# A grouped convolution in blocks of 16 positions of one group, the edges of two groups in one matrix, and tiles of one group of 16 rows

## What is computed

```python
# x (128, 32, 512), cond (128, 128), conv weight (32, 8, 9): 4 groups of 8 channels, 9 taps
y = conv_general_dilated(x, weight, (1,), [(4, 4)], ('NCH','OIH','NCH'), feature_group_count=4)
y = y + einsum('nd,od->no', cond, c_weight)[:, :, None] + bias[None, :, None]
base = einsum('btd,od->bto', y, base_W) + base_b            # 512 -> 512
logits = einsum('btd,nd->btn', y, router_W) + router_b      # 15 routes
p, i = top_k(softmax(logits), 8)
w = sum over k of p[k] * onehot(expert_map[i[k]])           # (.., 8 experts)
h = einsum('btd,erd->bter', y, A)                           # 8 experts x rank 16
out = x + base + einsum('bter,eor->bto', h * w[..., None], B) * 2
```

## Time and profile before

| | |
|---|---|
| median of 3 runs | 197.27 us (197.12 to 205.5) |
| profiled execution | 197.38 us, span 195.6 us |
| granted TensorE clock, mean | 0.991 |
| TensorE busy | 187.3 us, 96%, 1297 matmuls |
| VectorE busy | 161.1 us, 82% |
| ScalarE busy | 76.9 us, 39% |
| GpSimd busy | 139.1 us, 71% |
| moved | 27.66 MB, mean 141 GB/s |

### The profile page before, as it was taken

One profiled execution on the slowest core, in us unless ns is written; L12 is line 12 of the kernel. 1 busy time (PEld: TensorE's weight loads), 2 busy tenths in 40 slices (PEclk: granted clock), 3 DMA queues, 4 the chain that ended last, 5 costly groups with the idle time before them and its releaser, 6 DMA issues.

```text
span 195.6 us, 4329 instructions
## 1 busy us (share of the span) xinstructions
PE 187.3 (96%) x1297; PEld 180.1 (92%) x1297; DVE 161.1 (82%) x547; ACT 76.9 (39%) x197; POOL 139.1 (71%) x115
## 2 busy tenths in 40 slices
PE   7899699999999999999999999999999999998993
PEld 2788599999999999999999999999999999997992
DVE  0899987888889888889888889888898889775663
ACT  3674434434333444433334444343344443122210
POOL 4539796777887777777887777778877777943520
PEclk9999969999999999999999999999999999999999
DMA  5985442455444434445443335444334133333312
GB/s 180 312 292 214 111 140 80 159 167 162 146 124 124 152 116 153 162 162 157 125 140 123 134 130 162 162 162 147 137 110 150 71 86 111 107 107 109 111 54 107
DMA packets 19051, 27.66 MB, mean 141 GB/s; under 512 B 2144, under 2 KB 9696, under 8 KB 19040
## 3 DMA queue, kind: packets, MB, share of 16 engines
q1 hardware_dynamic: 18576, 27.05, 42.6%
q10 hardware_dynamic: 432, 0.48, 0.7%
q0 software_dynamic: 32, 0.01, 0.2%
HBM read 19.14 MB, written 8.39 MB: 141 GB/s over the span
## 4 chain that ended last, share of the span: by engine, by line
PE 83%; DVE 8%; DMA 4%; issue 2%; ACT 1%; DVEq 0%; ACTq 0%
PE wide_ps L516 53%; PE conv_banks L498 15%; PE wide_ps L540 10%; DMA wide_sb<-wide_w 2%; DMA x_in<-x_first 2%; PE hwt_bank L527 2%; PE conv_banks L516 1%; DVE terms L672 1%; DVE y_rows L647 1%; DVE xr L642 1%; DVE wide_lo L757 1%; DVE y L731 1%; DVE spread L703 0%; DVE expert_w L707 0%; ACT wide_hi L324 0%
## 5 line engine op out<-in xcount | busy, mean ns | idle before, releaser
L516 PE MATMUL wide_ps<-wide_hi,y_hi 128*128 128x400 f32 (+1 forms) x248 | 80.4, 329 | 1.1 <-DVE xr L642 0.8
L516 PE MATMUL wide_ps<-wide_lo,y_hi 128*128 128x400 f32 (+1 forms) x248 | 77.1, 315 | 0.0
L516 PE MATMUL wide_ps<-wide_hi,y_lo 128*128 128x400 f32 (+1 forms) x248 | 76.8, 314 | 0.0
L437 POOL TENSOR_TENSOR terms_lo<-terms,terms_hi 128x768 fp32r<-128x768 f32 x28 | 51.6, 1842 | 31.8 <-ACT terms_hi L345 31.8
L516 PEld LDWEIGHTS wide_ps<-wide_hi,y_hi 128*128 128x128 f32 x248 | 46.6, 189 | 3.5 <-issue 1.0
L516 PEld LDWEIGHTS wide_ps<-wide_lo,y_hi 128*128 128x128 f32 x248 | 46.9, 190 | 0.0
L516 PEld LDWEIGHTS wide_ps<-wide_hi,y_lo 128*128 128x128 f32 x248 | 46.6, 189 | 0.0
L432 POOL TENSOR_TENSOR xr<-xr,biases_sb 128x512 f32<-128x512 f32 x32 | 41.3, 1291 | 5.6 <-DMA xr<-x_rows 5.5
L443 POOL TENSOR_TENSOR y_lo<-y,y_hi 128x512 fp32r<-128x512 f32 x31 | 40.2, 1295 | 3.3 <-ACT y_hi L352 3.3
L359 ACT ACTIVATE hw_hi<-hwt_bank 128x128 fp32r<-128x128 f32 x31 | 8.6, 277 | 81.7 <-PE hwt_bank L527 81.7
L352 ACT ACTIVATE y_hi<-y 128x512 fp32r<-128x512 f32 x32 | 20.2, 632 | 17.9 <-PE wide_ps L516 16.8
(11 more groups left out here) (93 smaller groups left out, 256.3 us busy)
## 6 DMA issues: line engine op xcount, KB each, us to landing
xr<-x_rows SPq DMA_DIRECT2D x32, 256.0 KB, 2.7
out<-xr SPq DMA_DIRECT2D x31, 256.0 KB, 2.0
even<-x_even SPq DMA_DIRECT2D x28, 132.0 KB, 2.6
terms<-x_odd SPq DMA_DIRECT2D x28, 128.0 KB, 2.8
wide_sb<-wide_w SPq DMA_DIRECT2D x4, 328.0 KB, 5.1
x_in<-x_first SPq DMA_DIRECT2D x2, 260.0 KB, 4.3
x_in<-x_pair SPq DMA_DIRECT2D x1, 520.0 KB, 5.9
biases_sb<-biases SPq DMA_DIRECT2D x1, 263.5 KB, 4.3
```

The source lines that it names most:

```text
L437: nc.gpsimd.tensor_tensor(terms_lo[i % 2][:, :, :, :], terms[i][:, :, :, :], terms_hi[i % 2][:, :, :, :].bitcast(F32), ALU.subtract)\
L516: mm = nc.tensor.matmul(sums_of(t, k)[:, b, 0:columns[1] - columns[0]], a[k % 2][:, r, :], w[:, r, columns[0]:columns[1]], start=r == 0 an ...
```

## The change

A block is now 16 positions of the 8 channels of one group, which is 128 partitions again, and a tile is one group of 16 batches (16 x 32 blocks = 512 columns). Output block and input block have the same size, and since 9 taps reach only 4 positions to each side, the second matrix is nearly empty: shifted by 8 positions for the even groups, each output block needs its own input block (W_OWN) and, in one half of its positions only, a neighbour (W_REACH). Per tile there are two products of 256 columns, (W_OWN + W_REACH) on shared blocks and W_OWN on the loaded difference; the third product, the edge, is nonzero in one half of the output partitions only, and the edges of an even and an odd group lie in one matrix (W_QUARTERS): one product for two tiles. So an even tile has nine matmuls of 256 columns, an odd one six.

VectorE subtracts one term a tile (`difference`), and one edge term every second step (`edge`, both operands from SBUF). `condition` waits for the whole convolution and is three additions, each waiting for the one before: the shared sum and the condition; the other sum and the shared rows; the edge sum and the shared rows of 64 partitions. `turn` waits for the last. The common sum's own semaphore is gone. The edge sums lie in the bank of the transposed `hw`, and `turn_hw` now waits for the condition of tile t + 3. ScalarE and GpSimd split 512 + 256/2 elements a tile instead of 768. SyncE loads 256 KB a tile and 256 KB of edges for two, after the low parts of the same step.

The start is written anew: four tiles directly, convolution weights in five pieces (14 matrices instead of 4), condition weights and the expert map loaded on ScalarE's queue, the comparison with the experts' numbers by eight small operations on VectorE, placed ahead of the first condition, and `hw_low(0)` in step 0. Steps 1 to 28 have one convolution each. Keep-warm matmuls between the first convolutions and the first front are 3 instead of 4.

```diff
+            def conv(t, g, p):
+                h = g % 2
+                pe.wait_ge(terms_lo_ready, t - START + 1)
+                parts = [(conv_ps[:, h, 0, :, :], W_SUM[g], terms_hi[h][:, 1], terms_lo[h][:, 1]),
+                         (conv_ps[:, h, 1, :, :], W_OWN[g], terms_hi[h][:, 0], terms_lo[h][:, 0])]
                 if h == 0:
+                    pe.wait_ge(y_rows_ready, t)
+                    parts.append((edge_ps, W_QUARTERS[g // 2], edge_hi, edge_lo))
+                else:
+                    pe.wait_ge(y_rows_ready, t - 1)
...
             def turn_hw(t, k):
+                if from_tile(t, 1) and up_to_tile(t, TILES - 4):
+                    pe.wait_ge(y_rows_ready, t + 4)
...
-                if from_tile(t, 1) and up_to_tile(t, TILES - 5):
-                    conv(t, k, p)
+                if from_tile(t, 1) and up_to_tile(t, TILES - 4):
+                    conv(t + 3, (k + 3) % GROUPS, p + 2)
...
+            def condition(t, g, q):
+                h = g % 2
+                shared, other = 1 - h, h
+                rows = y_rows[h]
+                reached = slice(EDGE, P) if h == 0 else slice(0, EDGE)
+                dve.wait_ge(conv_done, t + 1)
+                c = cond_sb[:, g, bass.ds(q * Q, Q)]
+                nc.vector.tensor_tensor(rows[:, :, shared, :], conv_ps[:, h, 0, :, :],
+                                        c.unsqueeze(2).to_broadcast([P, Q, MK]), ALU.add)\
                     .then_inc(common_ready, 1)
+                dve.wait_ge(common_ready, t - START + 1)
+                nc.vector.tensor_tensor(rows[:, :, other, :], conv_ps[:, h, 1, :, :],
+                                        rows[:, :, shared, :], ALU.add).then_inc(own_ready, 1)
+                dve.wait_ge(own_ready, t - START + 1)
+                nc.vector.tensor_tensor(rows[reached, :, shared, :], edge_ps[reached],
+                                        rows[reached, :, shared, :], ALU.add)\
                     .then_inc(y_rows_ready, 1)
...
+            def difference(t, i):
+                dve.wait_ge(odd_ready, t - START + 1)
+                nc.vector.tensor_tensor(terms[i][:, 0, :, :], terms[i][:, 0, :, :], odd_ps,
+                                        ALU.subtract).then_inc(differences_ready, 1)
+            def edge(p, j):
+                dve.wait_ge(edges_loaded[j], (p - START // 2 - j) * 8 + 16)
+                nc.vector.tensor_tensor(edges[j][:, 0, :, :], edges[j][:, 0, :, :],
+                                        edges[j][:, 1, :, :], ALU.subtract).then_inc(edge_ready, 1)
...
             wide_low(0)
+            dve.wait_ge(map_ready, 1)
+            for e in range(E):
+                nc.vector.tensor_scalar(is_expert[:, e, :], map_f[:, :], float(e), None,
+                                        ALU.is_equal).then_inc(is_expert_ready, 1)
+            bias_condition(0)
+            condition_first(0)
+            turn(0, 0)
...
+            def step(t, k, p, q):
+                if isinstance(t, int) and t < START - 2:
+                    condition_first(t + 2)
+                elif up_to_tile(t, TILES - 3):
+                    condition(t + 2, (k + 2) % GROUPS, q + (k + 2) // GROUPS)
...
+                if up_to_tile(t, TILES - 5):
+                    difference(t + 4, k)
+                    if k % 2 == 1 and up_to_tile(t, TILES - 7):
+                        edge(p + 3, 1 - k // 2)
...
# SyncE, in each step
                     sync.wait_ge(terms_lo_ready, t + 1)
+                    load_terms(t + 8, k % URING)
+                    if k % 2 == 0:
+                        sync.wait_ge(edge_lo_ready, p + 1)
+                        load_edges(p + 4, k // 2)
```

More of the change, by code:

```diff
@@ L470, in keep_warm, with conv_first @@
                     nc.tensor.matmul(bank, zeros[:, 0:P], zeros[:, :], start=True, stop=True)
-            def conv_first(sums, i, h, products):
+            X_HIGH, X_W_REST, X_REST = (conv_hi, x_hi), (conv_lo, x_hi), (conv_hi, x_lo)
+            def conv_first(t, products=(X_HIGH, X_W_REST, X_REST)):
                 for w, a in products:
-                    for b in range(BLOCKS):
-                        mm = nc.tensor.matmul(sums, w[:, h, b, :], a[i][:, h, :, b:b + M],
-                                              start=w is conv_hi and a is x_hi and b == 0,
-                                              stop=a is x_lo and b == BLOCKS - 1)
-                return mm
@@ new lines @@
+    blocks = []
+    for g in range(GROUPS):
+        first = (1 - g % 2) * BP // 2
+        own = quads[:, g, :, :, first:first + BLKI * BP].reshape(N // Q, Q, CG, BLKI, BP)
+        blocks.append(own.transpose(0, 4, 2, 1, 3).reshape(N // Q, P, Q, BLKI))
+    blocks = np.stack(blocks, axis=1)
+    units, edges = [], []
+    for g in range(0, GROUPS, 2):
+        even, odd = blocks[:, g], blocks[:, g + 1]
+        units += [np.stack([even[..., 0:BLK:2], even[..., 1:BLK:2]], axis=2),
+                  np.stack([odd[..., 2:BLKI:2], odd[..., 1:BLKI:2]], axis=2)]
+        edges.append(np.stack([
+            np.concatenate([even[:, :EDGE, :, 2:BLKI:2], odd[:, EDGE:, :, 0:BLK:2]], axis=1),
+            np.concatenate([even[:, :EDGE, :, 1:BLK:2], odd[:, EDGE:, :, 1:BLKI:2]], axis=1)],
+            axis=2))
@@ L860 @@
+    units = np.stack(units[:GROUPS], axis=1).reshape(TILES, P, 2, Q, MK)
+    edges = np.stack(edges, axis=1).reshape(TILES // 2, P, 2, Q, MK)
     w = np.asarray(L0_cond_weight)
-    conv = np.zeros((BP, CH, HALVES, BLOCKS, BP, CH), w.dtype)
-    for b in range(BLOCKS):
+    conv = np.zeros((W_ALL, BP, CG, BP, CG), w.dtype)
+    for g in range(GROUPS):
+        own_w = w[g * CG:(g + 1) * CG].transpose(2, 1, 0)
+        later = g % 2 * BP // 2
         for s in range(BP):
             for r in range(BP):
-                tap = BP * b + s - r
+                tap = s - r + later
@@ L866 @@
                 if 0 <= tap < TAPS:
[L867 to L874 removed]
+                    conv[W_OWN[g], s, :, r] = conv[W_SUM[g], s, :, r] = own_w[tap]
```

529 lines of the change are left out of this document (262 added, 267 removed).

## The result

| | before | after |
|---|---|---|
| median | 197.19 us (196.28 to 205.5) | 204.65 us (204.61 to 204.67, 4 runs) |
| ratio, 95% interval | | 1.0394 [1.0359, 1.0429] |
| profiled execution, span | 197.38, 195.6 | 204.66, 202.5 |
| first front matmul of tiles 1, 2, 3, 4 | 17.33, 27.08, 33.56, 39.08 | 20.29, 26.55, 34.48, 40.46 |
| of tile 28 | 172.11 | 178.95 |

The kernel became 3.9% slower, and the medians lie 7.5 us apart. (The 205.5 is one slow execution, which the ratio leaves out.) The span grew by 6.9. Until the front of tile 4 it is 1.38 us late, the 24 steps from there to tile 28 take 138.49 us instead of 133.03 (+5.46), and the end 23.55 instead of 23.49. The other 0.4 lies outside the span (2.16 instead of 1.78).

The account below looks back on a forecast made before the run. The prediction took two loops of nearly one length, TensorE's work (5.54 us) and the ring (5.48), as bounds. 195.6 + 0.6 (loop) - 0.2 (start) = 196.0 span, plus 1.8 around it: 197.8 us, range 194.6 to 201.2.

Parts of the forecast that it names:

- the start: Everything up to the third front: front 1 later, at 19.4, front 2 earlier, at 25.2; - 0.2 us, between - 3 and + 3.
- the end: The work after the loop: the same as before, 0 us.
- The ring: Front matmuls, logits, routing, output addition, next front: 5.48 us a step, not shortened by the diff, limiting any gain to 1.6.
- the rival that TensorE binds: Rival (a), in the loop: TensorE binds, all 5.0 us of removed matmuls come out, 192.6 us; chance 0.07.
- VectorE's chain with an edge difference: From the condition's start through additions, turn and differences to the logits, with the edge difference every second step: 2.59 us.
- VectorE's chain without it: From the condition's start through three additions, turn and differences to the logits, in steps without an edge difference: 2.26 us.
- The slower rival: Rival (b): dependent additions (0.11 gaps) or a turn of 0.85 cost more, 202 us; decides from 0.28 on; chance 0.13.
- When the condition can start: VectorE sees the convolution's end 5.74 us after the front's start with nine matmuls, 5.38 with six.
- two loops: In the kernel before: TensorE's own work, 5.54 us, and the path front matmuls, logits, routing, output addition, next front, 5.48.
- The map's delay: In the start: the expert map's conversion is ready at 9.2, so the first turn ends at 11.9 against 9.82 before.
- The 0.3 that I allowed for the clock: In the start: 0.3 us for a lowered TensorE clock, since the new step 2 has idle time like that before.
- The signs that the prediction gave for too short a chain: In the loop: the turn's row over 0.75 us, or gaps between the three additions over 0.1.

Follow-up runs that it names:

- twice a step: Kernel before the change, with both differences of a unit reading the odd blocks from SBUF instead of their PSUM copy: 221.49 us, ratio 1.1237.
- the last kernel: Changed kernel with edge differences and map comparisons on GpSimd, the first addition early, and the output addition ahead of the hw product: 191.91 us, 0.9741 against the kernel before.

## Why the prediction was wrong

The forecast was 197.8 us, within 194.6 and 201.2. It was 204.65, above the range. Of the 6.85 us between, 4.9 are in the loop (+ 5.46 measured, + 0.6 in the sum), 1.6 in the start (+ 1.38, - 0.2), 0.06 in the end and 0.4 outside the span. In order of its steps:

**The ring: right.** The removed matmuls are worth nothing while it stands (1.000 without them, in the old order), and the rival that TensorE binds, with 5.0 us to gain, fell. By the rule that the prediction names from the Trainium skill ("Perfetto Trace Analysis", Identifying the Most-Contended Engine) 5.0 us would have come out. The trace doesn't bear it out: the measured gain of the matmuls alone is 0. In the kernel after, half of the steps without an edge difference are the ring, 5.53.

**VectorE's chain with an edge difference: the term that was mis-sized.** I had 2.59 and it is 3.10. The edge difference was put at 0.395, the mean of a row with one operand in PSUM. It measured 0.78 in the step shown, 0.81 on average, and that is 0.39 of the 0.51. The diff said "both operands from SBUF", and I took the price of the other kind, gave it no bound above, and listed GpSimd's rows without asking what runs at the same time. Over 14 pairs, 0.41 a pair would be 5.7 us if nothing else bound; taking the edge differences off VectorE gave 3.0 us, 1.3 of them in the start, since the next bound was near.

**VectorE's chain without it: mis-sized too, by less.** 2.26 in the sum. Where nothing else holds it back (the kernel without the edge difference) it is 2.46 in one half of the steps and 2.55 in the other. The three additions take 0.42 each and not 0.41, 0.395, 0.395 (+ 0.07), the gaps between them are 0.04 and not 0.03, the turn starts in one half of the steps 0.12 after the last addition, and the difference starts 0.04 behind the turn where I had an overlap of 0.07. Why these two differ stays open. In the step shown from 98.36 the logits wait for the front as well, so its 2.55 isn't the chain alone, and the steps without an edge difference lost only some 0.05 each. The slower rival said that it decides from 0.28 more on that chain; it was 0.20 to 0.29 here and up to 0.51 with an edge difference. A longer chain did decide, so its chance of 0.13 was too small, but neither of its two causes made most of that: the additions and their gaps made 0.1 to 0.2, the turn nothing, and the edge difference it didn't name.

**When the condition can start: mis-sized.** I had 5.74 after the front for nine matmuls. It is 5.92, read from the kernel with no edge difference: the last matmul starts at 5.48 instead of 5.42, mostly since the front's first matmul costs 0.26 and not 0.22, and VectorE starts 0.16 after its end (96.38 to 96.54) instead of 0.04. The 0.04 holds for the logits, which start so soon after the front's last matmul (93.06 to 93.09 in that run), but not for the condition's addition. The pair by this path is then 5.92 + 2.46 + 2.86 + 0.16 = 11.40 and not 11.06. In the kernel after the two paths meet: the convolution's last matmul is over at 98.20, the addition could start at 98.36, and VectorE is free at 98.29.

**VectorE's own queue: a loop that I didn't close.** I read two loops. VectorE's order of one step is a third: chain plus routing, 3.10 + 2.86 = 5.96, is the whole step with an edge difference, and TensorE then only follows. Even with my own numbers it would have been 2.59 + 2.91 = 5.50, as near to the bound as the ring, so that any mis-sized operation went straight to the end.

**The start: the sign was wrong.** - 0.2 in the sum, + 1.38 measured. The map's delay was nearly right: 9.58 for the end of its conversion against 9.2, the first turn over at 12.12 against 11.9. The front of tile 1 came at 20.29, not at 19.4, tile 2's at 26.55 (25.2), tile 3's at 34.48 (33.1). The first steps have the same long operations: the two low parts of `wide` took 2.69 instead of 1.59, the first edge difference 0.71 and that of step 3 1.07. Without edge differences on VectorE the front of tile 4 comes at 39.18, nearly the old 39.08. The 0.3 that I allowed for the clock was not needed: it was granted in full from 26 to 28 too, where it had been 0.50 before.

**What was right and cost nothing in the loop:** the turn with its runs of 8 (0.712, before 0.707); the end (+ 0.06); the transfers, SyncE's order, ScalarE and GpSimd's slack, for none of which TensorE or VectorE waits from 60 to 160 us; the transposition of `hw`, whose new wait shows once, in step 2 (1.40 us). The signs that the prediction gave for too short a chain (the turn over 0.75, gaps over 0.1 between the additions) stayed away, although the chain was too short: they watched the wrong operations.

**Where the 7.5 us went,** in the order in which the runs took them away: edge differences off VectorE 3.0 (204.65 to 201.69), the first addition early 3.5 (to 198.2), the map's comparisons off VectorE 1.4 (to 196.82), 7.8 in all and 0.4 more than the medians had lost. The profiled executions divide this in start and loop (us):

| | front of tile 4 | from there to the front of tile 28 |
|---|---|---|
| before | 39.08 | 133.03 |
| after | 40.46 | 138.49 |
| no edge difference | 38.86 | 136.86 |
| its operand in PSUM | 39.74 | 136.93 |
| edge differences on GpSimd | 39.18 | 136.89 |
| and the first addition early | 41.19 (the late load) | 132.80 |
| and the comparisons on GpSimd | 38.24 | 132.79 |

In the loop the price of the edge difference is thus 1.6 us and the late first addition behind it 4.1. The division depends on this order, since the first two bounds lie behind one another; that the early addition alone would give 3.5 with the edge differences in place wasn't tried, and the missing wait there (98.36 against 98.29) speaks against it.

## What to carry to other kernels

Before pricing an operation, look for a row with its operands in the same memories and with the same neighbour at work, not only of its shape; if it is VectorE's and both operands lie in SBUF, ask what GpSimd does at that time, and if nothing shows it, carry as the upper bound the length of GpSimd's instruction more (here 1.3 us; the longest edge difference beside one instruction took 1.07). Close the loop of each engine's own queue as well as the ring through several engines, since with three loops within about 1% (5.48, 5.50 and 5.54 here) shortening one gains nothing, and lengthening one costs almost all that is added. An operation that waits for the last of several products, where it needed only the first, adds the others' duration to its chain, and a semaphore with a bank of its own gave 3.5 us back here.

## What the runs showed of the hardware

- A VectorE difference of 128 x 256 with both operands in SBUF took 0.42 us while GpSimd was idle and 0.55 to 1.07 beside its work (mean 0.81; twice a step 0.98). In the kernel after all 14 ended 0.27 to 0.29 us after the end of the GpSimd instruction beside which they started. With one operand in PSUM it took 0.41 beside the same instruction. Where it was done twice a step, GpSimd paid as well (1.44 instead of 1.29).
- Eight comparisons of 15 elements, with one SBUF operand each, took 0.70 us alone and 4.10 beside GpSimd's work. That is 0.43 more for each, as much as the edge difference of 256 elements lost (0.39): in these two cases the loss went by the instruction, not by its size. On GpSimd itself the eight took 3.99.
- An addition over 64 partitions takes what one over 128 does: 0.422 and 0.425.
- How soon VectorE starts after TensorE isn't one number. Idle and waiting, it started the condition's addition 0.15 to 0.19 us after the end of the convolution's last matmul (96.38 to 96.54), but the logits 0.03 to 0.04 after the end of the front's last (93.06 to 93.09, idle 0.23 before). Ends of matmuls are modelled in the trace; why the two differ stays open.
- TensorE's first front matmul costs 0.26 us after an idle time. In the last kernel, where TensorE is never idle, it costs 0.26 in every second step, where it starts 0.16 to 0.17 after the start of the matmul before it, and 0.18 in the others, where that is 0.11. A delay of 0.05 is enough.
